# A vision layer with routed experts: the token step reordered, the scatters split around the values product, and the two norms merged

## The reference: what is computed

```python
h = patches @ W.T + b                                   # 2048 x 192
h = h + attention(layernorm(h))                         # 12 heads of 16, rotary, causal
u = layernorm(h)
t = u * rsqrt(mean(u * u) + 1e-5) * norm_scale          # rmsnorm
g = t @ gate_w.T + gate_b;  top_vals, top_idx = top_k(g, 4)
comb = one_hot(top_idx) weighted by softmax(top_vals)   # 2048 x 16
y = swiglu(t @ mlp1_w.T + mlp1_b) @ mlp2_w.T + mlp2_b   # for each expert
return h + (u + sum over experts of y * comb)
```

## Time and profile before

| | |
|---|---|
| runs | 519.35, 524.19, 524.24 us; median 524.19 |
| profiled execution | 524.42 us, span 522.6 us |
| busy over the span | PE 439.6, ACT 311.3, DVE 306.1, POOL 254.0 us |
| indirect DMAs on POOL | 64 into routed_rows (63.1 us), 79 into out_rows (124.6 us) |
| DMA | 49.73 MB, mean 95 GB/s |

### The profile page before, as it was taken

The page is one execution under the profiler, slowest core; times in us unless marked ns, Lnnn a source line. Parts: engine busy times, 40 slices in busy tenths (PEclk is TensorE's granted clock), DMA queues, the critical chain, the costliest instruction groups (busy, mean ns, idle before and its releaser), DMA issues. The chain is left out here.

```text
span 522.6 us, 14562 instructions
## 1 busy us (share of the span) xinstructions
PE 439.6 (84%) x3869; PEld 389.9 (75%) x3870; DVE 306.1 (59%) x1049; ACT 311.3 (60%) x832; POOL 254.0 (49%) x302
## 2 busy tenths in 40 slices
PE   3888888778877765428999999999999999999990
PEld 2667667566565544217999999999999999999980
DVE  0466976787878765543555555555555555555550
ACT  1256756566666554116767677777777777777730
POOL 1113476766666655750233645544444444445443
PEclk9989999999999856558999999999999999999996
DMA  8964454555547111223323535444334444333222
GB/s 224 262 172 146 132 178 146 150 147 162 167 140 210 51 49 39 78 75 97 75 47 57 78 62 72 67 63 64 58 55 62 63 59 60 57 56 39 28 30 30
DMA packets 42107, 49.73 MB, mean 95 GB/s; under 512 B 6387, under 2 KB 33507, under 8 KB 42052
## 3 DMA queue, kind: packets, MB, share of 16 engines
q1 hardware_dynamic: 27604, 34.35, 24.4%
q0 software_dynamic: 14448, 14.72, 18.5%
HBM read 30.82 MB, written 18.23 MB: 94 GB/s over the span
## 5 line engine op out<-in xcount | busy, mean ns | idle before, releaser
L1206 POOL DMA_INDIRECT out_rows<-x_sb,row_to x79 | 124.6, 1577 | 161.6 <-DMA out_rows<-x_sb,row_to 68.9
L590 PE MATMUL bank<-rT,w_now 128*128 128x128 f32 x948 | 123.7, 281 | 0.3 <-ACT rT L635 0.3
L590 PEld LDWEIGHTS bank<-rT,w_now 128*128 128x128 f32 x948 | 114.8, 193 | 5.2 <-ACT rT L635 0.5
L635 ACT ACTIVATE w_now<-w_sb 128x1158 f32 x79 | 92.5, 1171 | 26.9 <-issue 20.2
L725 ACT ACTIVATE k_spread<-bank,w_now 128x128 f32<-128x128 f32 x237 | 70.0, 373 | 56.0 <-PE bank L598 56.0
L1079 DVE TENSOR_TENSOR v_sb<-bank,w_now 128x384 f32<-128x384 f32 x79 | 44.0, 557 | 78.7 <-PE bank L598 59.8
L612 PE MATMUL bank<-w_sb,p_spread 128*128 x474 | 83.9, 327 | 0.4 <-DVE x_sb L1102 0.4
L612 PEld LDWEIGHTS bank<-w_sb,p_spread 128*128 128x128 f32 x474 | 76.1, 190 | 0.8 <-issue 0.7
L1146 POOL DMA_INDIRECT routed_rows<-packet,row_i x64 | 63.1, 986 | 24.2 <-issue 22.5
L1092 DVE SCALAR_TENSOR_TENSOR p_spread<-k_spread,v_sb 128x384 f32<-128x384 f32 x79 | 44.1, 559 | 35.2 <-ACT k_spread L725 30.5
L598 PE MATMUL bank<-rT,w_now 64*128 64x128 f32 x948 | 64.1, 281 | 0.0
(11 more groups left out here) (182 smaller groups left out, 613.5 us busy)
## 6 DMA issues: line engine op xcount, KB each, us to landing
x_sb<-patches SPq DMA_DIRECT2D x16, 384.0 KB, 3.6
w_sb<-w SPq DMA_DIRECT2D x32, 192.0 KB
w_sb<-w SPq DMA_DIRECT2D x16, 288.0 KB
w_sb<-w SPq DMA_DIRECT2D x64, 48.0 KB
wtok_sb<-routed_rows SPq DMA_DIRECT2D x25, 106.0 KB
routed_rows<-zero_row SPq DMA_DIRECT2D x17, 106.0 KB
out_rows<-h SPq DMA_DIRECT2D x16, 96.0 KB
out_rows<-x_sb,row_to POOLq DMA_INDIRECT x79, 3.6
```

The costliest lines, as they stand in the source:

```text
L590: last = mm(dst[:, c * P:(c + 1) * P], w[:, a:a + P], t[:, part, :], start=(start and c == 0), stop=(not start and c == ICH - 1))
L635: return nc.scalar.activation(dst, src, ACT.Copy)
L1206: G.indirect_dma_start(out=out, out_offset=bass.IndirectOffsetOnAxis(ap=row_to[:, b % NY:b % NY + 1].bitcast(U32), axis=0), in_=y_out[b % ...
```

## The change

The token step is rearranged on all four engines, with the same products on PE.

- **Norms.** Both roots of tile t come from one variance: roots[0] is (var + T_EPS)^-0.5, which with T_SCALE on the norm's scale is layernorm and rmsnorm in one (rms of x2 is var / (var + eps)), and roots[1] is (var + eps)^-0.5. POOL makes both in one addition and one pow over two columns, then gain = roots[1] + 1 and shift = -mean * roots. ACT makes two rows from h1 by Identity with scale and bias: normed, and the base h1 * gain + shift. x2, its Square, the third root, and POOL's residual are gone. DVE multiplies normed by the scale straight into the packet, of which there are now four (PACKETS) instead of two; the copies of row and weights into it are gone, and two conversions (of the chosen experts' numbers and of the row places) are folded into their users.
- **PE.** Order now: turn xn, q, k, t, then qk, rank, turn weights, project, embed, gate, scores, bias, v, values. Embed comes behind qk and the projection; the values product is the last of the step.
- **ACT.** Exp (prob), v copy and yT copy move to the start of the next step.
- **DVE.** The order is new throughout; norm (xn) is near the end of the step.
- **POOL.** Tile n - 7 is scattered in step n, one step later than before: two of its four scatters behind normalise, then both root pairs, then a wait for the values product of the same step (`pv_done`), then the other two. In the last steps the rest follows (step 18: tiles 11 and half of 12; step 19: the other half and tile 13; then one tile a step).

Removed functions and lists stand in the kernel above and are left out here.

```diff
+T_EPS, T_SCALE = EPS * EPS / (1.0 + EPS), (1.0 + EPS) ** -0.5
...
+PACKETS = 4
...
-            return (t - buf) * 8 * TOPK
+            return (t - buf) * 16 * TOPK // PACKETS
...
             def step(tile, seen, n):
                 par = n % 2
+                if tile(1) is not None:
+                    bank_free(("xnT_ready", seen(1, 1)), ("tT_ready", seen(5, 1)))
+                    turn_halves(tile(1), ps_xT, xn, "xn_ready", "xn_turned")
+                if tile(2) is not None:
+                    bank_free(("qT_ready", seen(2, 1)), ("top_i_ready", seen(5, 1)))
+                    turn_halves(tile(2), ps_qT, qk[:, 0:DIM], "qk_ready", "q_turned")
+                    bank_free(("k_spread_ready", seen(2, 1)))
+                    turn_halves(tile(2), ps_kT, qk[:, DIM:2 * DIM], "qk_ready", "k_turned")
+                if tile(5) is not None:
+                    bank_free(("tT_ready", seen(5, 1)), ("xnT_ready", seen(1)))
+                    turn_halves(tile(5), ps_tT, packet[tile(5) % PACKETS], "t_row_ready", "t_turned")
+                if tile(1) is not None:
+                    bank_free(("rope_s_ready", seen(1, 1)))
+                    qk_product(tile(1))
+                if tile(6) is not None:
+                    bank_free(("place_ready", seen(6, 1)), ("yT_ready", seen(3, 1)))
+                    rank(tile(6))
+                    bank_free(("combT_ready", seen(6, 1)), ("sc1_ready", seen(2, 1)))
+                    turn_weights(tile(6))
+                if tile(4) is not None:
+                    bank_free(("h1_ready", seen(4, 1)), ("v_ready", seen(1, 1)))
+                    project(tile(4))
                 if tile(0) is not None:
                     t = tile(0)
-                    bank_free(("h0_ready", seen(0, 1)), ("combT_ready", seen(6, 1)))
-
+                    bank_free(("h0_ready", seen(0, 1)), ("base_full", seen(6, 1)))
                     embed(t, par, 16 * (t // 2 + 1) if isinstance(t, int) else (t - par) * 8 + 16)
                 if isinstance(tile(0), int) and tile(0) == 0:
                     pe.wait_ge(consts_in, 16)
                     pe.wait_ge(wsmall_in, 16 * 7)
                     pe.wait_ge(setup_pool, 3)
                     pe.wait_ge(setup_act, 2)
...
+                    pe.wait_ge(setup_dve, 3)
                 if tile(5) is not None:
...
+                    bank_free(("top_i_ready", seen(5, 1)), ("qT_ready", seen(2)))
                     gate(tile(5))
                 if tile(2) is not None:
-                    bank_free(("sc1_ready", seen(2, 1)))
+                    bank_free(("sc1_ready", seen(2, 1)), ("combT_ready", seen(6)))
                     scores(tile(2))
...
                 if tile(6) is not None:
-                    bank_free(("base_full", seen(6, 1)), ("qT_ready", seen(2)))
+                    bank_free(("base_full", seen(6, 1)), ("h0_ready", seen(0)))
                     experts_bias(tile(6))
                 if tile(1) is not None:
                     bank_free(("v_ready", seen(1, 1)), ("h1_ready", seen(4)))
                     v_product(tile(1))
+                if tile(3) is not None:
+                    bank_free(("yT_ready", seen(3, 1)), ("place_ready", seen(6)))
+                    values(tile(3), (n - 3) % 2)
...
             def step(tile, seen, n):
...
+                if tile(3) is not None:
+                    t = tile(3)
+                    act.wait_ge(s["sc2_ready"], t + 1)
+                    wait(act, s["p_pair_ready"], 2 * t)
+                    wait(act, s["rsum_ready"], t)
+                    nc.scalar.activation(prob[:], sc2[:], ACT.Exp).then_inc(s["prob_ready"], 1)
                 if tile(1) is not None:
                     move(tile(1), xnT[0:HALF], ps_xT, "xn_turned", "v_done", "xnT_ready")
                 if tile(2) is not None:
                     move(tile(2), qT[:], ps_qT, "q_turned", "scores_done", "qT_ready")
+                    t = tile(2)
+                    act.wait_ge(s["v_done"], t + 1)
+                    wait(act, s["pv_done"], t - 1)
+                    copy(v_sb[:, t % 2, 0:DIM], ps_v).then_inc(s["v_ready"], 1)
+                if tile(5) is not None:
+                    move(tile(5), tT[0:HALF], ps_tT, "t_turned", "gated", "tT_ready")
+                if tile(4) is not None:
+                    move(tile(4), yT[:], ps_yT, "pv_done", "proj_done", "yT_ready")
                 if tile(2) is not None:
                     spread_keys(tile(2))
-                if tile(5) is not None:
-                    move(tile(5), tT[0:HALF], ps_tT, "t_turned", "gated", "tT_ready")
+                if tile(6) is not None:
+                    move(tile(6), combT[:], ps_cT, "comb_turned", "b2_done", "combT_ready")
                 if tile(3) is not None:
                     spread_probs(tile(3))
-                if tile(6) is not None:
-                    move(tile(6), combT[:], ps_cT, "comb_turned", "b2_done", "combT_ready")
                 if tile(4) is not None:
                     t = tile(4)
...
+                    act.wait_ge(s["shift_ready"], t + 1)
+                    act.wait_ge(s["gain_ready"], t + 1)
+                    wait(act, s["t_row_ready"], t)
+                    nc.scalar.activation(normed[:], h1[:], ACT.Identity, bias=shift[:, 0:1], scale=roots[:, 0:1]
+                                         ).then_inc(s["normed_ready"], 1)
+                    nc.scalar.activation(h0[:, t, :], h1[:], ACT.Identity, bias=shift[:, 1:2], scale=gain[:]
+                                         ).then_inc(s["base_ready"], 1)
                 if tile(5) is not None:
                     t = tile(5)
                     act.wait_ge(s["top_d_ready"], t + 1)
                     wait(act, s["top_w_ready"], t)
                     nc.scalar.activation(top_e[:], top_d[:], ACT.Exp, accum_out=esum[:]).then_inc(s["top_e_ready"], 1)
...
+            V.tensor_scalar(nscale_bc[:], nscale_bc[:], T_SCALE, None, ALU.mult).then_inc(setup_dve, 1)
...
             def norm2(t):
...
+                dve.wait_ge(s["normed_ready"], t + 1)
+                wait(dve, scattered[t % PACKETS], rows_out(t, t % PACKETS))
+                V.tensor_tensor(packet[t % PACKETS][:, 0:DIM], normed[:], nscale_bc[:], ALU.mult
+                                ).then_inc(s["t_row_ready"], 1)
...
-            def top_float(t):
+            def mark_experts(t):
                 dve.wait_ge(s["top_i_ready"], t + 1)
...
                 V.tensor_tensor(onehot[:], const("expert").unsqueeze(1).to_broadcast(pke),
-                                top_f[:].unsqueeze(2).to_broadcast(pke), ALU.is_equal
+                                top_i[:, 0:TOPK].unsqueeze(2).to_broadcast(pke), ALU.is_equal
                                 ).then_inc(s["onehot_ready"], 1)
...
             def combine(t):
                 dve.wait_ge(s["onehot_w_ready"], t + 1)
-                wait(dve, s["comb_turned"], t)
-                V.tensor_reduce(comb[:], onehot_w[:].rearrange("p k e -> p e k"), AX_X, ALU.add
+                V.tensor_reduce(packet[t % PACKETS][:, W_AT:W_AT + EXPERTS], onehot_w[:].rearrange("p k e -> p e k"), AX_X, ALU.add
                                 ).then_inc(s["comb_ready"], 1)
...
+            def note_token(t):
+                V.tensor_copy(packet[t % PACKETS][:, ID_AT:ID_AT + 1].bitcast(I32), token_i[:, t:t + 1]
                               ).then_inc(s["token_ready"], 1)
...
             def place_sum(t):
+                buf = t % 2
                 dve.wait_ge(s["onehot_r_ready"], t + 1)
...
+                if t >= 2:
+                    dve.wait_ge(scattered[(t - 2) % PACKETS], rows_out(t + PACKETS - 2, (t - 2) % PACKETS))
+                with nc.allow_low_precision("row numbers are whole"):
+                    V.tensor_reduce(row_i[buf][:], onehot_r[:], AX_X, ALU.add).then_inc(s["row_i_ready"], 1)
...
-                par5, par6 = (n - 5) % 2, (n - 6) % 2
-                at(3, prob_sum)
                 at(6, mark_experts)
                 at(6, choose_experts)
+                at(3, prob_sum)
                 at(6, top_weights)
                 at(3, prob_inverse)
                 at(3, prob_inverse_own)
                 at(6, weigh_experts)
-                at(5, norm3, par5)
                 at(6, combine)
...
+                at(6, note_token)
+                at(1, rope_products)
+                at(3, turn_probs)
                 at(4, attn_add)
-                at(0, embed_aggr)
-                at(3, turn_probs)
                 at(4, attn_stats)
                 at(6, place_all)
                 at(4, attn_aggr)
-                at(0, norm)
+                at(1, rope_add)
                 at(6, place_chosen)
                 at(6, place_sum)
-                at(6, place_whole, par6)
+                at(0, embed_add)
+                at(0, embed_stats)
                 at(5, top_max)
-                at(1, rope_products)
-                at(4, norm2)
+                at(0, embed_aggr)
+                at(5, top_index)
```

(68 more changed lines are left out.)

148 lines of the change are left out of this document (26 added, 122 removed).

## The result

The changed kernel took 499.27 us (median of 4, 498.07 to 500.74) against 524.22 us beside it: ratio 0.9536 [0.9463, 0.961]. I had said 500. Ratios here leave out the few executions that were slower at a lower granted clock (three of the ten of b4_values_last, one of them 743.98 us at 0.552; its trace and that of b1_wait are such ones). The profiled execution took 500.74 us, with a span of 499.0. The table splits both spans in the same way, at the starts of the values products of steps 8 and 16, 0.93 us behind the start of the last one, and at the first expert product.

What follows compares the result with a forecast made beforehand. No engine was full; late values reports and a loop through POOL's root were taken to bound the steps. Steps -15.7, fill -3, emptying -6, last stretch 0: -24.7 from 524.42 gives 500 us (492 to 508; whole range 490 to 517).

Steps and rivals of the forecast that it cites:

- The late report: Token steps: a values product starting with POOL's scatters is reported 2.8 to 4.6 us late, holding up ACT and DVE.
- The second loop: Token steps: scatters, root rms, t_row, statistics, roots, scatters also fill 11.76 us, so undoing either loop alone brings little.
- The size of a step: Full steps: 11.76 us falls to 9.8, set by DVE; over eight steps -15.7 us (-9.3 to -23.7).
- 0.85 left over, 0.4 and 0.6 for the new order: DVE idle per step: 0.85 us staying without the bias wait, 0.4 for exposed q/k products, 0.6 for embed, gate, scores.
- the packet copy that I priced them by: ACT: two Identity copies priced at 0.355 us each, like the packet copy; ACT stays near 7.2 us, costing nothing.
- POOL's new wait: POOL, each step: waiting for the values holds up two scatters and the next p_pair, 0.5 us spare, so no cost.
- Fill and emptying: Steps before and after the eight full ones: fill -3 us (+2 to -6), emptying -6 (-2 to -9).
- The last stretch: Last values product to first expert row: two more scatters offset by fewer roots, stays POOL's, 0 us (-1 to +3).
- my two signs that the forecast had failed: Forecast fails if a step exceeds 10.6 us or the stretch before the first expert row grows over 3 us.
- Rival 1: Values report late whatever POOL does; the new wait closes a 10.6 us loop: 514 us (509 to 518), chance 0.17.
- Rival 2: First scatter pair delays projection and embed reports: 12.8 us steps, 536 us (529 to 545), deciding from 2 us; chance 0.11.
- Rival 3: ACT: Identity between Exps forces two table loads a step, some 11.7 us: 524 us (519 to 529), chance 0.06.

Runs made afterwards that it cites:

- b4_values_last: Kernel before with one move in PE's list, the values product behind bias and v, POOL untouched: 512.9 us, ratio 1.0022 to the kernel before.
- b1_wait: Kernel before plus one line, POOL waiting for the same step's values product ahead of its four scatters: 541.19 us, ratio 1.0542 to the kernel before.
- d2_four_last: Changed kernel without waits for the values, all four scatters behind both roots, for the tile just placed: 566.61 us, ratio 1.0832 to the kernel before.
- c1_before: Kernel before, no edit, traced again in another group of runs: 511.24 us, ratio 0.9998.
- c3_norms: Kernel before with only the change's norms, all orders, packet copies and scatters as before: 495.06 us, ratio 0.9677 to the kernel before.
- d3_half_step: Changed kernel without waits, scatter pairs exchanged so the just-placed tile's first two go behind the roots: 519.87 us, ratio 0.9935 to the kernel before.
- b3_both: Kernel before with the change's norms and POOL's wait for the values ahead of its four scatters: 517.46 us, ratio 1.0112 to the kernel before.
- d1_four_first: Changed kernel without waits, all four scatters behind p_pair, then both roots: 519.02 us, ratio 0.9926 to the kernel before.
- a1_no_wait: Changed kernel without both of POOL's waits for the values product: 491.0 us, ratio 0.959 to the kernel before.

## Why the prediction was right

**The late report.** The step "when the values product starts together with the scatters, its report comes 2.8 to 4.6 us late" holds on a 524 chip: one pair beside it costs xnT 1.7 us against the like kernel on the 511 chip (3.17 and 1.49), four cost 4.5 in d2_four_last, and with the wait in the changed kernel no report of a product was "remote". As a rule for every chip it falls: c1_before has the same overlap and 0.93 us. One trace could not show that; that the same kernel could have no late report on another chip was in none of my rivals. The Trainium skill, SBUF — State Buffer, "Who interferes with whom", lets GpSimd contend for ports with DVE alone. Nothing in the 511 traces is against it; the late reports of the 524 traces are not accounted for by it, and whether ports have to do with them no run shows.

**The second loop.** "DVE's t_row needs the root rms, which POOL makes only after its scatters" is so in the kernel's order. But that this loop "fills the 11.76 us as well" was a wrong reading of the earlier trace rows: rms ends at 139.83 there, t_row starts at 140.40 and waits for nothing. In the whole trace on the 524 chip t_row waited for rms once, for 0.2 us; in that on the 511 chip 12 times, for 18.0 us. So the late reports set the 11.76 us, and the second loop, at 10.8 us, stood behind them. Each is worth something by itself: the late reports 7.9 us in eight steps (before to c1_before), the norms on a 511 chip 10.2 more (86.25 to 76.09, c3_norms), 3.2 to 3.6% of the whole. My sentence that undoing either loop alone would bring little is wrong. The norms also take 0.22 us of work a step off DVE and 0.62 off POOL; how much of the 10.2 us is that, and not the loop, was not taken apart. On a 524 chip neither part was tried alone.

**The size of a step.** 9.51 us against 9.8 forecast. DVE idles 1.38 us a step, where I had 1.9 (0.85 left over, 0.4 and 0.6 for the new order); which of the three was too large is not shown. Nor does DVE's list alone set the step: without POOL's wait it falls by 0.37 us on a 511 chip. The copies by Identity take more than the packet copy that I priced them by, 548 and 534 ns and not 355; ACT is busy 7.40 us of the 9.51, and no run shows whether they cost time. Groups by shape, 82.79 to 158.87: count, busy us, mean ns, idle before.
```profile
L1134 POOL TENSOR_TENSOR roots<-ve,power 128x2 f32<-128x2 f32 x8 | 5.8, 726 | 0.6
...
L694 ACT ACTIVATE normed<-h,shift,roots 128x192 f32<-128x192 f32 x8 | 4.4, 548 | 10.5 <-POOL shift L1137 10.5
L696 ACT ACTIVATE h<-h,shift,gain 128x192 f32<-128x192 f32 x8 | 4.3, 534 | 0.0
...
L885 DVE TENSOR_TENSOR packet<-normed,nscale_bc 128x192 f32<-128x192 f32 x8 | 2.8, 349 | 0.0
```

**POOL's new wait.** I costed it at nothing. On a 511 chip leaving it out gains 8.5 us (POOL stood 1.2 us a step for it, and the next p_pair and roots stand behind the scatters that it holds back). Between the two traces 3.0 us of this lie in the eight steps (9.41 us and 9.04), 1.9 in the emptying and 0.8 in the last stretch; 1.8 lie in the expert loop, where there is no such wait, and I can't account for those. On a 524 chip the changed kernel has 0.9536 and the nearest kernel without the wait (d3_half_step) 0.9935, with 17.3 us of waits on "remote" and a step of 11.2 us; that one also exchanges the pairs, so not all of the 4% is shown to be the wait's. The changed kernel without its waits was not run on a 524 chip.

**Fill and emptying** came out at -4.1 and -6.6 us (forecast -3 and -6). The kernel before, without late reports, has 1.5 and 4.1 us less in them by itself.

**The last stretch** is the term that was mis-sized: 0 forecast, +3.0 measured, at the upper end of what I allowed. It is also one of my two signs that the forecast had failed, growth by over 3 us (3.04 by the split of the table); the other, a step over 10.6 us, stayed far off. My "it stays POOL's" was the wrong step. DVE makes the table of slots there by 23 short instructions, beside the last scatters. In the kernel before they already took 7.4 us on the 524 chip:
```profile
223.01 0.17 DVE L1034 TENSOR_SCALAR cnt_i<-bank 128x16 int32<-128x16 f32 x1
...
230.22 0.15 DVE L1034 TENSOR_SCALAR of_tile<-of_tile 128x1 f32<-128x1 f32 x1
```
That is about when the last scatter ended (230.69). In the changed kernel they take 10.7 us and end at 205.22, 2.2 us behind the last scatter. They start as long after the last values product as before (18.3 and 18.0 us), so their 3.4 us more are what lengthened the stretch: the first expert product now comes 7.9 us behind the last scatter's end, where it was 5.9. The first of them and some that waited, in the changed kernel:
```profile
194.48 0.17 DVE L1009 TENSOR_SCALAR cnt_i<-bank 128x16 int32<-128x16 f32 x1
...
197.33 0.17 DVE L1009 TENSOR_TENSOR jumped<-passed,jump 128x16 f32<-128x16 f32 x1 [1.61 <-remote]
...
202.99 0.16 DVE L1009 SCALAR_TENSOR_TENSOR of_tile<-of_tile 128x1 f32<-128x1 f32 x1 [1.25 <-DVE of_tile L1009]
203.68 0.16 DVE L1009 SCALAR_TENSOR_TENSOR of_tile<-of_tile,cst 128x1 f32<-128x1 f32 x1 [0.53 <-DVE of_tile L1009]
205.07 0.15 DVE L1009 TENSOR_SCALAR of_tile<-of_tile 128x1 f32<-128x1 f32 x1 [1.24 <-DVE of_tile L1009]
```
The waits between these instructions of one engine are 0.4 to 1.6 us. The last two of them end 0.7 and 2.1 us behind the last scatter's end on POOL (202.99), so the lateness outlasts the issuing. Why there is more of it in the changed kernel is open. On a 511 chip the same chain in the changed kernel:
```profile
194.04 0.16 DVE L1009 TENSOR_SCALAR cnt_i<-bank 128x16 int32<-128x16 f32 x1
...
196.30 0.15 DVE L1009 TENSOR_SCALAR of_tile<-of_tile 128x1 f32<-128x1 f32 x1
```
2.4 us (2.6 in the kernel before), over 6 us ahead of the last scatter's end at 202.53. There the stretch is POOL's, as I had said: the first expert product comes 4.7 us behind the last scatter's end in both kernels, and it grew by 0.9 us only (29.66 to 30.53). The **expert loop** grew by 2.1 us on both kinds of chip (286.0 to 288.1, 286.91 to 288.97); the change leaves it alone, without the waits it is 287.2, with the norms alone 287.3, and I don't know the cause.

**The rivals.** Rival 1 (late whatever POOL does) is out: with the wait, what reads the values product or the one behind it waited for nothing remote on a 524 chip, and on a 511 chip yT is on time with the scatters beside. Its loop, values to scatters to p_pair, is real and is what b1_wait and b3_both ran into. Rival 2 has its mechanism: reports of other products do come late beside scatters. The changed kernel's pair costs little there, as its step is 9.51 us on a 524 chip and 9.41 on a 511 one, far under the 2 us from which I let it decide. Four scatters (d1_four_first) cost 1.1 us at half_s. With the roots behind them, for which ACT waits 3.0 us a step, the step is 11.2 us and nearly the whole gain is lost; how much of that is late reports was not taken apart. Rival 3 is out: two table loads in the first 245 us, one of them ahead of the Silu, as in the kernel before, although Identity now stands between the Exps. The Trainium skill, ScalarE: Activation LUTs, "Table sets: the hidden batching unit", has identity in every set, and the trace agrees.

## What to carry to other kernels

A stall that a profile calls "remote" may not belong to the kernel: trace the unchanged kernel a second time, on another chip, before an order is built around it. That an engine reads another's result shows a loop, but only a wait for it in the trace shows that the loop holds the step. Where POOL issues indirect DMAs all along, the order of its list decides twice, by what stands behind them on POOL and, on some chips, by whose reports fall beside them. On the 511 chips the best orders had the root of a norm not behind all four scatters; on a 524 chip all four behind the roots, beside the values product, was the slowest order of all (d2_four_last, 566.61 us). A wait that shields one engine is paid by everything queued behind it, here up to 8.5 us where there was nothing to shield.

## Of the hardware

- One kernel, unchanged, has two levels, 511 and 524 us, at nearly the same granted clock (0.928 and 0.932). On a 524 chip, beside POOL's scatters, what waits for another instruction's end is released late: a values product's readers by 2.8 us in the kernel before, by 1.7 beside one pair (d3_half_step) and 4.5 beside four (d2_four_last), dependent instructions of DVE by 0.4 to 1.6 each (changed kernel), up to 2.1 us behind the last scatter's end. On a 511 chip nothing of it shows in nine traces. What makes the difference stays open.
- The length of a step doesn't tell the granted clock, for the same products: 1.00 in steps of 9.0 us (a1_no_wait), 0.98 in steps of 11.76 (the kernel before), 0.85 in steps of 11.5 (b3_both), 0.82 in steps of 15.7 (d2_four_last). What decides between the 11.76 and the 11.5 was not looked into.
